# Attention with the exponentials of a unit added on GpSimd: one ones product a unit, queries in fp32, loads in quarters

## The reference

```python
def _L0_xattn_ref(query, key, value, ...):          # 16 heads of 32
    Q = split_heads(query @ Wq.T + bq)
    K = split_heads(key @ Wk.T + bk)
    V = split_heads(value @ Wv.T + bv)
    scores = jnp.einsum('bhqd,bhkd->bhqk', Q, K) / np.sqrt(Hd)
    attn = jax.nn.softmax(scores, axis=-1)
    out = jnp.einsum('bhqk,bhkd->bhqd', attn, V)
    return out.transpose(0, 2, 1, 3).reshape(B, S, D) @ Wo.T + bo
x = x + _L0_xattn_ref(_layernorm(x), ctx_1024, ctx_1024, ...)
x = x + _L0_ffn_ref(_layernorm(x), ...)              # 8 experts, the best 2 of each token
```

## Time and profile before

| | |
|---|---|
| median of three runs | 1845.72 us |
| the profiled execution, its own time | 1853.42 us |
| its span | 1851.7 us |
| PE, DVE, ACT, POOL busy | 91%, 69%, 35%, 25% |
| granted TensorE clock, mean | 0.957 |
| start of unit 0's turned maxima, of unit 31's | 69.42 us, 1026.91 us |

### The profile page before, as it was taken

One profiled execution on the slowest core, in us unless ns is written; L12 is line 12 of the kernel. 1 busy time (PEld: TensorE's weight loads), 2 busy tenths in 40 slices (PEclk: granted clock), 3 DMA queues, 4 the chain that ended last, 5 costly groups with the idle time before them and its releaser, 6 DMA issues. The chain is left out here.

```text
span 1851.7 us, 30932 instructions
## 1 busy us (share of the span) xinstructions
PE 1687.5 (91%) x10405; PEld 1249.3 (67%) x10405; DVE 1281.3 (69%) x2267; ACT 645.6 (35%) x1253; POOL 460.8 (25%) x643
## 2 busy tenths in 40 slices
PE   4699999998999989999999826999999999999996
PEld 3456555565555555555554326999999999999995
DVE  4576667666775766676656486876888768876874
ACT  3254353352433543533524303322333224322321
POOL 2112112112121121121211102333343343433322
PEclk8899999999999999999999966999999999999998
DMA  5323233332341432333312142223344335324322
GB/s 185 88 80 108 62 98 113 103 102 60 95 111 52 121 98 65 98 113 98 92 46 70 41 162 76 67 86 131 125 162 157 97 127 183 111 86 138 119 72 80
DMA packets 93813, 188.74 MB, mean 102 GB/s; under 512 B 25168, under 2 KB 26192, under 8 KB 93648
## 3 DMA queue, kind: packets, MB, share of 16 engines
q1 hardware_dynamic: 66736, 108.24, 19.1%
q0 software_dynamic: 26912, 78.47, 14.1%
HBM read 204.19 MB, written 37.36 MB: 130 GB/s over the span
## 5 line engine op out<-in xcount | busy, mean ns | idle before, releaser
L600 DVE TENSOR_REDUCE negmax<-max_ps 128x2 f32<-128x1024 f32 x256 | 311.5, 1217 | 151.6 <-PE max_ps L381 150.2
L485 ACT ACTIVATE pt<-work 128x512 f32<-128x512 f32 x512 | 277.9, 597 | 329.1 <-PE work L393 327.2
L1198 PE MATMUL gu_ps<-xgT_hi,wg_hi 128*128 128x256 f32 x1248 | 355.7, 285 | 0.0
L1198 PE MATMUL gu_ps<-xgT_hi,wg_lo 128*128 128x256 f32 x1248 | 352.5, 282 | 0.0
L1198 PE MATMUL gu_ps<-xgT_lo,wg_hi 128*128 128x256 f32 x1248 | 352.2, 282 | 0.0
L381 PE MATMUL max_ps<-ks,qs 96*128 96x512 f32 x512 | 191.0, 455 | 61.1 <-DVE negmax L600 42.9
L1198 PEld LDWEIGHTS gu_ps<-xgT_hi,wg_hi 128*128 128x128 f32 x1248 | 236.2, 189 | 0.0
L1198 PEld LDWEIGHTS gu_ps<-xgT_lo,wg_hi 128*128 128x128 f32 x1248 | 236.1, 189 | 0.0
L1198 PEld LDWEIGHTS gu_ps<-xgT_hi,wg_lo 128*128 128x128 f32 x1248 | 235.9, 189 | 0.0
L381 PEld LDWEIGHTS max_ps<-ks,qs 96*128 96x128 f32 x512 | 85.7, 198 | 143.4 <-issue 74.7
L1258 ACT ACTIVATE sig<-gate 128x256 f32<-128x256 f32 x156 | 65.1, 417 | 330.0 <-DVE gate L1310 330.0
(11 more groups left out here) (193 smaller groups left out, 2959.9 us busy)
## 6 DMA issues: line engine op xcount, KB each, us to landing
raw_g<-w_gate_up SPq DMA_DIRECT2D x39, 2048.0 KB
raw_d<-w_down SPq DMA_DIRECT2D x39, 1024.0 KB
ks<-k_hi SPq DMA_DIRECT2D x256, 64.0 KB, 2.2
qs<-q_hi SPq DMA_DIRECT2D x256, 64.0 KB, 2.7
bd<-b_down SPq DMA_DIRECT2D x39, 256.0 KB
x_in<-x SPq DMA_DIRECT2D x8, 1024.0 KB, 5.8
ctxT_raw<-ctx_t SPq DMA_DIRECT2D x8, 1024.0 KB, 6.4
ks<-k_lo POOLq DMA_DIRECT2D x128, 64.0 KB, 2.3
```

The costliest lines, as they stand in the source:

```text
L485: e.activation(pt[k % 2][:, h, :], in_work("exp", u, k, h)[:, :], ACT.Exp, scale=scale).then_inc(exped.sem, 1)
L600: e.tensor_reduce(negmax[:, u % 2, n:n + 2], max_ps[:, :, :], AX.X, ALU.max, negate=True).then_inc(maxed.sem, 1)
L1198: ins = e.matmul(gu_ps[n % GU_BANKS][:, part, :], wg[s][pw][:, k, cols], xgT[s][px][:, k, :], start=(k == 0 and m == 0), stop=(k == KD - 1 ...
```

## The change

- Four tiles of exponentials of a unit are added on POOL into a new tile `acc` (`add_weights`: two heads an instruction, 128x1024, six instructions a unit), and `sum_weights` runs once a unit, on `acc`, into a `work` bank, in round 2 of the next step. ACT copies only this bank, into `inv`.
- `o_ps` is now two banks, one for even and one for odd units, and `normalise` multiplies straight from them. `sum_ps` is gone. ACT's exponentials wait for the add of the tile that had their buffer before.
- Queries are projected by four float32 products instead of twelve float32r ones; `wq` and `xT` are not split.
- `x_in`, `ctx_raw` and `x2` are loaded in quarters, statistics and `ln1` run one tile a round, and the four transposes of batch 0 go to `max_ps` and `o_ps`, which are idle then.
- The table: values of unit 0 are projected after the first maxima, `x` of batch 1 loads a step later, and normalisations, output, `ln2` and logits have other rounds.

```diff
-        o_sum = sb("o_sum", [P, 2, S])
+        acc = sb("acc", [P, GROUP, S])
+        inv = sb("inv", [P, S])
...
-        o_ps = psum("o_ps", [P, S])
-        sum_ps = psum("sum_ps", [P, S])
+        o_ps = [psum(f"o_ps{i}", [P, S]) for i in range(2)]
...
+                u, j = (s, r - 2) if r > 1 else (s - 1, r + 6)
+                if u in units and j > 1:
+                    at(r, ("add", u, j // 2, j % 2))
                 if r == 1 and s - 1 in units:
-                    at(r, ("weigh", s - 1, T - 1), ("sum", s - 1, T - 1))
+                    at(r, ("weigh", s - 1, T - 1))
+                if r == 2 and s - 1 in units:
+                    at(r, ("sum", s - 1))
                 if r % 2 and r > 1 and s in units:
-                    at(r, ("weigh", s, (r - 3) // 2), ("sum", s, (r - 3) // 2))
+                    at(r, ("weigh", s, (r - 3) // 2))
...
+                for t, r in enumerate((6, 6, 7, 7) if c == 1 else (3, 3, 4, 5)):
+                    at(r, ("norm", s - 1, t))
+                if c == 0:
+                    at(7, ("out", b - 1, 0))
+                if c == 1 and last:
+                    for t in range(1, T):
+                        at(2 * t - 1, ("out", b - 1, t))
...
+            later = b + 2 if c == 3 and b >= 0 else 1 if s == 0 else B
+            if later in bs:
+                for t in range(T):
+                    at(1 + t, ("load_x", later, t))
+                    at(3 + t, ("stats", later, t))
+            later = b + 1 if c == 0 and b >= 1 else 1 if s == 1 else B
+            if later in bs:
+                for t in range(T):
+                    at(t, ("ln1", later, t))
...
+        idle = {("turn_x", 0, t): bank for t, bank in enumerate((max_ps[:, 0, :], max_ps[:, 1, :], o_ps[0][:, :], o_ps[1][:, :]))}
...
+                    for k in range(C):
+                        ins = e.matmul(to[:, :], wq[:, k, cols], xT[:, k, :], start=(k == 0), stop=(k == C - 1))
...
-                    if u:
-                        e.wait_ge(copied.sem, copied[u - 1, 0])
+                    if u >= 2:
+                        e.wait_ge(divided.sem, divided[u - 2, T - 1])
+                ins.then_inc(weighed.sem, 1)
+
+            def sum_weights(u):
+                to = take("sum", u)
+                e.wait_ge(added.sem, added[u, T - 1, 1])
                 for h in range(GROUP):
-                    ins = e.matmul(sum_ps[HD * h:HD * (h + 1), :], ones[:, :], pt[k % 2][:, h, :], start=(k == 0), stop=(k == T - 1))
-                ins.then_inc(weighed.sem, 1)
+                    ins = e.matmul(to[HD * h:HD * (h + 1), :], ones[:, :], acc[:, h, :], start=True, stop=True)
+                ins.then_inc(summed.sem, 1)
...
+                    u_before, k_before = TILES[n - 2]
+                    e.wait_ge(added.sem, added[u_before, max(k_before, 1), h // 2])
                 e.activation(pt[k % 2][:, h, :], in_work("exp", u, k, h)[:, :], ACT.Exp, scale=scale).then_inc(exped.sem, 1)
...
-                e.tensor_tensor(oT[:, c, cols], o_sum[:, 0, cols], o_sum[:, 1, cols], ALU.mult).then_inc(divided.sem, 1)
...
+                e.tensor_tensor(oT[:, c, cols], o_ps[u % 2][:, cols], inv[:, cols], ALU.mult).then_inc(divided.sem, 1)
...
+            def add_weights(u, k, p):
+                heads = slice(2 * p, 2 * p + 2)
+                e.wait_ge(exped.sem, exped[u, k, 2 * p + 1])
+                if k == 1:
+                    if u:
+                        e.wait_ge(summed.sem, summed[u - 1])
+                    e.tensor_tensor(acc[:, heads, :], pt[0][:, heads, :], pt[1][:, heads, :], ALU.add).then_inc(added.sem, 1)
+                else:
+                    e.wait_ge(added.sem, added[u, k - 1, p])
+                    e.tensor_tensor(acc[:, heads, :], acc[:, heads, :], pt[k % 2][:, heads, :], ALU.add).then_inc(added.sem, 1)
...
+            def load_x(b, t):
...
+                e.dma_start(x_in[:, t, :], rows_of(x, b)[:, t, :]).then_inc(x_loaded[t].sem, 16)
```

More of the change, by code:

```diff
@@ L76, in attention_stage @@
         w, w_raw = {}, {}
-        for n in "kqv":
+        for n in "kv":
             w[n], w_raw[n] = split(f"w{n}", [P, C, D])
+        wq = sb("wq", [P, C, D])
         ctxT, ctx_raw = split("ctxT", [P, C, S])
         wo = sb("wo", [P, C, D])
-        xT = [sb(f"xT_{part}", [P, C, S], F32R) for part in ("hi", "lo")]
+        xT = sb("xT", [P, C, S])
         x_at = nc.sbuf_base
@@ L172, in step @@
                     at(3, ("low", u, "q"))
-                    if s == -2:
-                        at(3, *[("split", "v", k) for k in range(C)])
                     at(4, ("v", u, 0))
@@ L199, in step @@
                 at(3, ("turn_xln", b - 1, 2))
-                at(4, ("logits", b - 1, 0), ("turn_xln", b - 1, 3))
-                at(6, ("logit_sum", b - 1, 0), ("logits", b - 1, 1))
+                at(4, ("logits", b - 1, 0))
+                at(5, ("turn_xln", b - 1, 3))
+                at(6, ("logit_sum", b - 1, 0))
+                at(7, ("logits", b - 1, 1))
+            later = b + 2 if c == 3 and b >= 0 else 1 if s == 0 else B
[7 more added lines that the diff above has]
+                    at(t, ("ln1", later, t))
             if c == 3:
-                if b + 2 in bs:
-                    at(0, ("load_x", b + 2))
-                    at(4, ("stats", b + 2))
-                    at(6, ("ln1", b + 2))
                 if b in bs:
-                    at(0, ("residual", b))
-                    at(4, ("bo", b))
+                    for t in range(T):
+                        at(4 + t, ("residual", b, t))
                 if last:
                     at(0, ("logit_sum", b - 1, 1))
+            if c == 0 and last:
+                for t in range(T):
+                    at(1 + t, ("bo", b - 1, t))
             return [key for keys in rounds for key in keys]
@@ L268, in attention_stage @@
         eps2_added, rstd2_made = Mark(sem("eps2_added"), TOKENS), Mark(sem("rstd2_made"), TOKENS)
-        bo_added = Mark(sem("bo_added"), bs)
+        bo_added = Mark(sem("bo_added"), TOKENS)
+        added = Mark(sem("added"), [(u, k, p) for u in units for k in range(1, T) for p in range(2)])
         at = {key: n for n, key in enumerate(ORDER)}
@@ L284, in attention_stage @@
                 over, end = (v_made, tuple(what)), ("v_out", *what)
-            elif kind == "turn_x":
-                over = xT_lo_made, tuple(what)
+            elif kind == "turn_x" and what[0]:
+                over = xT_made, tuple(what)
+            elif kind == "sum":
+                over = copied, what[0]
             elif kind == "out":
@@ L299, in attention_stage @@
         ring = Ring(uses)
-        in_work = lambda *key: work[ring.bank[key]]
+        idle = {("turn_x", 0, t): bank for t, bank in enumerate((max_ps[:, 0, :], max_ps[:, 1, :], o_ps[0][:, :], o_ps[1][:, :]))}
+        in_work = lambda *key: idle[key] if key in idle else work[ring.bank[key]][:, :]
         def on_pe(e):
             def take(*key):
-                if ring.before[key]:
+                if key not in idle and ring.before[key]:
                     mark, event = ring.before[key]
@@ L508, in on_act @@
                     exp_one(*what)
-                elif kind == "sum" and what[1] == T - 1:
-                    copy_sums(what[0])
+                elif kind == "sum":
+                    copy_sums(*what)
                 elif kind == "turn_max":
@@ L521, in on_act @@
                 elif kind == "turn_x":
-                    x_hi(*what)
+                    x_copy(*what)
                 elif kind == "turn_xln":
@@ L615, in normalise @@
                 e.wait_ge(inverted.sem, inverted[u, t])
-                e.tensor_tensor(oT[:, c, cols], o_sum[:, 0, cols], o_sum[:, 1, cols], ALU.mult).then_inc(divided.sem, 1)
-            ln1_stats(0)
-            ln1(0)
+                e.tensor_tensor(oT[:, c, cols], o_ps[u % 2][:, cols], inv[:, cols], ALU.mult).then_inc(divided.sem, 1)
+            for t in range(T):
+                ln1_stats(0, t)
+            ln1_mean(0)
+            for t in range(T):
+                ln1(0, t)
             for kind, *what in ORDER:
@@ L638, in on_dve @@
                     ln1_stats(*what)
+                    if what[1] == T - 1:
+                        ln1_mean(what[0])
                 elif kind == "ln1":
@@ L644, in on_dve @@
                     ctx_lo(*what)
-                elif kind == "turn_x":
-                    x_lo(*what)
                 elif kind == "logit_sum":
@@ L690, in on_pool @@
                     stack_lo(*what)
-                elif kind == "stats":
-                    ln1_rstd(*what)
+                elif kind == "stats" and what[1] == T - 1:
+                    ln1_rstd(what[0])
+                elif kind == "add":
+                    add_weights(*what)
                 elif kind == "out":
```

165 lines of the change are left out of this document (83 added, 82 removed).

## The result

The changed kernel takes 1916.24 us (median of 4 runs, 1912.04 to 1921.74) against 1846.60 us of the kernel before (1843.57 to 1849.05) on the same chip. The ratio is 1.038, 95% interval 1.0345 to 1.0414: 70 us slower, where 11.7 us faster was forecast. The profiled execution took 1921.74 us, 68.3 more than the one of before.

The account below looks back on a forecast made before the run. Attention was taken as bound by PE's program order, with PE also waiting for DVE's reductions. Seven batches -2 us, start -13.6, end +4: -11.6 off the 1845.72 median gives 1834 us; range 1796 to 1868 (forecast's own 1815 to 1850).

Parts of the forecast that it names:

- the port term: Attention: GpSimd adds block DVE instructions with SBUF inputs, 1.15 us per meeting; +1.2 us a batch, bounds 0 and +11.
- The slower rival: POOL's reads stop DVE on the path, at `ctxT_lo`, `ln2` (c=1 to c=2) and `ln1` (c=0); 1866 to 1898 us; chance 0.20.
- PE's work: Attention on PE: fewer ones groups -2.7 us a unit, fp32 queries +0.75; net -7.7 us a batch.
- the clock: PE at 1.2 GHz after long waits costs 2.2 us a batch; half goes, -1.1, bounds 0 and -2.2.
- the old waits: PE's 8.5 us a batch of waits for DVE reductions and `q_hi` go: -6.8 and -1.7 us.
- new waits: PE waits for DVE in short rounds of c=3, c=0 and from c=1 into c=2, by a walk of rounds; +15.8 us a batch.
- Start: Attention's start: first scores -4.5 us, earlier `x` load -8.0, one unit without other waits -1.1; together -13.6 us.
- the rival that I gave 0.06: Quarters of `x` land no sooner behind SP's stacks; DVE waits 1.5 us a batch in c=3; 1844 us; chance 0.06.
- End: Last unit: six adds, the ones product, its copy and a normalisation precede the output; +4 us, bounds 0 and +9.
- Adds: GpSimd's `acc` adds take 2.3 us each, bounds 2.3 and 4.6; cost on the path 0 while under 3 us.
- its own test: Expected signs: PE about 85% busy, reduction waits 14 to 18 us a batch, `ctxT_lo` and `ln1` maxima near 2.8 us.
- three signs of being wrong: Waits under 10 us a batch, `acc` adds over 3 us, or DVE instructions that read PSUM stretching too.

Follow-up runs that it names:

- ln1_early: Changed kernel with the fourth tile of `ln1` normalised in round 2 of unit c=0 instead of round 3; 1866.96 us, ratio 1.0108.
- adds_wait: Changed kernel with GpSimd waiting for its own previous add ahead of each acc and bo add; 1876.92 us, ratio 1.0171.
- low_by_sp: Changed kernel with the DMAs of `k_lo` and `q_lo` issued by SyncE instead of GpSimd; 1906.77 us, ratio 1.0313.
- The first two benches: Separate small programs: one DVE instruction beside rows of GpSimd adds, with or without waits between them; `tensor_scalar` 0.55 us alone, 2.0 to 2.1 beside adds.
- spread_2: spread with statistics and `ln1` in other rounds, and the last unit's ones products a tile without GpSimd adds; 1817.38 us, ratio 0.9834.
- q_fp32: Kernel before with only the query change: four fp32 products for twelve fp32r ones, `wq` and `xT` unsplit; 1856.28 us, ratio 1.0057.
- spread: Changed kernel with waits between GpSimd's adds, earlier `ln1` and `x` loads, moved statistics and output products, one normalisation a round; 1834.32 us, ratio 0.9927.

## Why the prediction was wrong

**The step that failed** is the port term, "+1.2 us; bounds 0, and five each stopped a full add, +11". It assumed that "an instruction that meets an add waits 1.15 us on average", one add at the most. The earlier trace rows couldn't tell more: there the bo add was a single long instruction, and its end was the row's end too. Measured, one `ln1` a batch stood through four adds: 6.7 us of stretch, 8.7 us of PE wait. ln1_early takes it away and gives back 49 us, adds_wait and low_by_sp remove it in two other ways. The wait lay inside the term's bounds by luck of size; the value taken and the mechanism were wrong. The slower rival named the right engine pair and one right place ("`ln1` in c=0"), with 20% and 1866 to 1898; it too took single adds. Against it I had set that DVE idles 32% of a batch. But idle time between reductions is no slack: the stall stood in front of a reduction that PE waited for.

It is not the only miss. A batch grew by 9.8 us where -0.3 was forecast. By terms, measured minus forecast: the port term +7.5 (8.7 for 1.2), PE's work with the clock +8.3 (-0.5 for -8.8), the old waits +1.6 (6.9 for the 8.5 counted), the other new waits -7.4 (8.4 for 15.8); together +10.0 of the 10.1.

The Trainium skill, SBUF — State Buffer, "Who interferes with whom", lets whoever issues first keep the shared pair for its whole instruction, and the other blocks until then. The first two benches, without DMAs, agree (2.0 us); behind GpSimd's own DMA issue the row shows 7.20 and 14.21, so there the measurement decides.

**The clock.** I took 1.1 us a batch as given back. The granted clock fell from 0.97 to 0.90. By unit, over the six batches, it is 0.86, 1.00, 0.87 and 0.90 in c=0 to c=3 (0.98, 1.00, 0.97 and 0.94 before). In c=1, at full speed, the value products take 4.05 us a unit, in the other units of after 4.7 to 4.8, and the exponentials' scores 4.3 against 4.7 to 5.0. In ln1_early c=0 is back at 0.99 and the rest is 1.3 us a batch shorter: that much of the clock's price hangs on the long wait.

**PE's work, -7.7 a batch.** Mis-sized, and most of the gap goes with the clock. The rest column gives -0.5 in after and, where the mean clock is that of before (spread_2), -5.1. Values and ones a unit at full speed (c=1): 7.51 before, 5.06 after, so -2.45 for the -2.67 of the text, 0.9 us a batch less. The queries were right: +0.69 a unit in q_fp32, with 0.40 of it in the scores behind them, and in after 0.1 more in three of four units. In spread_2 values and ones give 8.8 us a batch for 10.7, and nearly all that is missing beyond the 0.9 stands in c=2, where the clock is still 0.91 (values and ones 6.04 us for 5.05 in c=1).

**Old waits.** The places were right: no wait for `q_hi` is left in the six batches, and the statistics and `ln1` no longer stand in one piece. The sum was too high. The 8.5 us come out only with the waits at both ends of the window (2.33 us at 428.37 and 0.79 at 555.14, which is the next batch's), and over the six batches the mean is 6.9; so 1.6 us a batch were given back that weren't there. **New waits, +15.8.** Too high. Without the stalled `ln1` 8.4 us are left in after: 1.5 and 1.6 at the end of c=1 (1.7 and 2.3 forecast), 1.8 and 0.6 in c=2 (2.4 and 1.5), 2.7 in c=3 (4.6), and in ln1_early 2.2 in c=0 (3.3). The places were right, the sizes of the walk were not; why PE waited less at each is not shown. Two of them as the trace has them:

```profile
514.98 0.73 PE L422 MATMUL max_ps<-ks,qs 96*128 96x512 f32 x2 [1.50 <-DVE negmax L640]
...
518.77 0.27 PE L428 MATMUL work<-ident,negmax 128*16 128x128 f32 x1 [1.59 <-DVE negmax L640]
```

**Start.** First scores at 35.40 us (-4.2 for -4.5) and unit 0's maxima -10.1 for -12.5. But unit 0 then lost 4.3 us, to the rival that I gave 0.06, x landing late:

```profile
78.47 0.69 DVE L578 BATCH_NORM_STATS2 stats<-x_in 128x6 f32<-128x512 f32 x1 [4.97 <-DMA x_in<-x]
...
80.34 1.12 PE L422 MATMUL max_ps<-ks,qs 96*128 96x512 f32 x2 [4.51 <-DVE negmax L640]
```

In spread the loads go out in rounds 0 and 1 for 1 to 4, the statistics come one round later, and the unit takes 22.0 for 27.1 us.

**End.** +5.2 us to the output product for +4; the ones product waited 3.51 us for the last add.

**Adds.** 2.36 to 2.39 us on average for the 2.3 forecast. Their own lateness cost next to nothing, as costed (the exponentials waited 15.2 us for an add in the whole program). `ctxT_lo`, which I had named as a sign with maxima near 2.8, reached 2.6 us, but its median stayed at 0.69.

**By its own test** the waits for the reduction, "14 to 18 us a batch", came out at 14.6 (17.1 with all others), but by two errors against each other, 8.4 for 15.8 and 8.7 for 1.2: that is luck. None of the three signs of being wrong appeared either. The one sign that told was `ln1`, 7.2 us for the "maxima near 2.8".

## What to carry to other kernels

Before work goes to GpSimd, list which DVE instructions such an add stops (here `tensor_scalar` from SBUF to SBUF and `tensor_tensor` with two SBUF inputs, but neither reciprocal nor `bn_stats`), and what GpSimd does just ahead of them: a DMA issue followed by ready adds shuts them out for the whole row, and what counts is whether a reduction that PE waits for stands behind. A wait of GpSimd for its own last add leaves 0.08 to 0.14 us between two adds and opens the row. An engine's idle share is no cover for a stall; walk the rounds, and take a single long instruction in a trace as no evidence on what happens between two.

## What the runs showed of the hardware

Not expected: behind a DMA issued by GpSimd, a `tensor_scalar` from SBUF to SBUF doesn't get in between GpSimd's adds until they end or GpSimd has to wait (7.20 us beside four adds, 14.21 beside eight, 0.55 alone), one DMA is enough, and DMAs of SyncE don't do it (1.40). Without such DMAs it gets in at the next seam, also where the adds overlap by 0.04 us (2.02). A `tensor_tensor` with two SBUF inputs stands the same way (7.46); reciprocal (3.35), `bn_stats` (0.69) and a sum that reads PSUM (0.69) take their own time behind the same DMAs. The add that it slips in front of is hardly longer (2.52 for 2.33 us). Why the DMA issue has this effect is not shown.
